# A fused cross-attention and feed-forward block on one core: the scores of batches 3 to 7 from fp16 parts

## What is computed

```python
def attention(k, v, q, Wk, Wv, bv, Wq, bq, Wo, bo):
    kp = k @ Wk.T;  vp = v @ Wv.T + bv;  qp = q @ Wq.T + bq
    probs = softmax(qp @ kp.T / sqrt(512))
    return probs @ vp @ Wo.T + bo
def ffn(x, w_gate, w_up, w_down):          # fp4(.): blocks of 16 rounded to the FP4 grid, scaled back
    h = silu(fp4(x) @ fp4(w_gate).T) * (fp4(x) @ fp4(w_up).T)
    return fp4(h) @ fp4(w_down).T
x = x + tanh(g_xattn) * attention(ctx, ctx, layernorm(x), ...)
x = x + tanh(g_ffn) * ffn(layernorm(x), ...)
```

## Time and profile before

| | |
|---|---|
| time, median of 3 runs (lowest to highest) | 863.45 us (861.89 to 864.26) |
| the profiled execution: its own time | 863.36 us |
| its span | 861.6 us |
| busy: PE, DVE, ACT, POOL | 850.2, 677.5, 375.3, 361.2 us |
| granted TensorE clock | 1.000 over the span |

### The profile page before, as it was taken

The page is one execution under the profiler, slowest core; times in us unless marked ns, Lnnn a source line. Parts: engine busy times, 40 slices in busy tenths (PEclk is TensorE's granted clock), DMA queues, the critical chain, the costliest instruction groups (busy, mean ns, idle before and its releaser), DMA issues.

```text
span 861.6 us, 11647 instructions
## 1 busy us (share of the span) xinstructions
PE 850.2 (99%) x4252; PEld 443.5 (51%) x4252; DVE 677.5 (79%) x1056; ACT 375.3 (44%) x661; POOL 361.2 (42%) x364
## 2 busy tenths in 40 slices
PE   8999999999999999999999999999999999999998
PEld 4566555544554455445544455445544554444443
DVE  5997989798988977878688858886787778877753
ACT  3666484643543344434443444334533544333320
POOL 4495448355543343334233433343333433333321
PEclk9999999999999999999999999999999999999999
DMA  9723110054334332622252225322332323333222
GB/s 308 275 71 114 27 50 14 14 120 103 70 85 104 59 59 46 130 59 58 51 114 54 59 42 124 66 58 59 64 78 58 47 60 75 60 58 64 59 46 70
DMA packets 149408, 67.45 MB, mean 78 GB/s; under 512 B 133108, under 2 KB 134502, under 8 KB 149352
## 3 DMA queue, kind: packets, MB, share of 16 engines
q1 hardware_dynamic: 149351, 66.72, 33.6%
HBM read 22.76 MB, written 8.39 MB: 36 GB/s over the span
## 4 chain that ended last, share of the span: by engine, by line
PE 69%; DVE 2%; issue 2%; ACT 1%; POOL 1%; DMA 0%; SPq 0%; POOLq 0%; ACTq 0%
PE banks L1505 44%; PE banks L1615 22%; PE banks L1499 1%; PE banks L1580 1%; PE banks L1579 1%; DVE arena L1081 0%; DMA arena<-h_parts 0%; DVE scal L1156 0%; DVE arena L1079 0%; POOL arena L527 0%; DVE stats L1121 0%; ACT h_parts L809 0%; ACT xn L735 0%; DVE ring L1243 0%; DVE h_parts L1238 0%
## 5 line engine op out<-in xcount | busy, mean ns | idle before, releaser
L1505 PE MATMUL banks<-wgu_hi,x_T 128*128 128x512 f16 (+1 forms) x1536 | 440.9, 361 | 0.0
L1505 PE MATMUL banks<-wgu_lo,x_T 128*128 128x512 f16 (+1 forms) x768 | 277.5, 361 | 0.0
L1615 PE MATMUL banks<-wd,arena 128*128 128x512 f16 x1056 | 234.6, 379 | 0.5 <-DMA arena<-h_parts 0.5
L1505 PEld LDWEIGHTS banks<-wgu_hi,x_T 128*128 128x128 f16 x1536 | 150.3, 98 | 153.4 <-issue 1.0
L1615 PEld LDWEIGHTS banks<-wd,arena 128*128 128x128 f16 x1056 | 103.3, 98 | 120.4 <-issue 0.9
L527 POOL TENSOR_TENSOR arena<-arena,h_r 128x1024 f32<-128x1024 f32 (+1 forms) x60 | 96.5, 1609 | 117.5 <-DVE h_r L1033 117.5
L527 POOL TENSOR_TENSOR arena<-arena,h_s 128x1024 f32<-128x1024 f32 x64 | 90.2, 1410 | 120.3 <-issue 89.4
L797 ACT ACTIVATE arena<-banks,scal 128x512 f32<-128x512 f32 (+1 forms) x96 | 62.1, 647 | 133.7 <-PE banks L1505 133.6
L1505 PEld LDWEIGHTS banks<-wgu_lo,x_T 128*128 128x128 f16 x768 | 75.1, 98 | 77.0 <-issue 1.3
L527 POOL TENSOR_TENSOR xwork<-xwork,x_s 128x512 f32<-128x512 f32 x32 | 33.9, 1059 | 174.3 <-DVE xwork L1081 174.3
L1079 DVE SCALAR_TENSOR_TENSOR arena<-arena 128x384 f32<-128x384 bf16 (+1 forms) x67 | 66.3, 989 | 26.2 <-ACT arena L676 26.2
(11 more groups left out here) (156 smaller groups left out, 949.9 us busy)
## 6 DMA issues: line engine op xcount, KB each, us to landing
ring<-in_x_dram SPq DMA_DIRECT2D x8, 1024.0 KB, 5.7
out_dram<-ring SPq DMA_DIRECT2D x32, 256.0 KB, 2.0
arena<-in_L_ffn_w_down_dram SPq DMA_DIRECT2D x4, 704.0 KB, 4.1
arena<-in_L_ffn_w_gate_dram SPq DMA_DIRECT2D x5, 512.0 KB, 10.8
arena<-in_L_ffn_w_up_dram SPq DMA_DIRECT2D x5, 512.0 KB, 11.0
ring<-in_L_xattn_Wk_dram SPq DMA_DIRECT2D x4, 256.0 KB, 6.0
ring<-in_L_xattn_Wq_dram SPq DMA_DIRECT2D x4, 256.0 KB, 6.8
wd<-in_ctx_dram SPq DMA_DIRECT2D x1, 1024.0 KB
```

The costliest lines, as they stand in the source:

```text
L1505: ended = e.matmul(at, l, r, start=(i == 0), stop=(i == len(terms) - 1))
L1615: ended = e.matmul(down_ps(t)[:, :], l, r, start=(k == 0 and i == 0), stop=(k == KH - 1 and i == 2))
```

## The change

From batch 3 on (`CUT = 3`) the layer norm's result and the keys are split in fp16 high and low parts, and the scores are made of high times (high, low) and low times high. What it does, engine by engine:

- PE: `att_turn` is gone for batches 3 to 7 (20 tiles). `att_scores` of such a tile is eight fp16 matmuls: four of 154 columns (the high part of xn against the keys' high and low columns side by side) and four of 77 columns (low against high). They stand in s = 1 alone: tile 0 at a1, 1 at a2, 2 and 3 at a3, in banks 5 and 6. `att_values` alternates banks 7 and 5. One transpose and one spread matmul are added in iteration 6 for the keys' power of two.
- ACT: `xn_copy` is replaced by `xn_high` (a cast of 128x512 from SBUF); the normed rows are made two tiles at a time. Once, in iterations 6 and 7: four `key_high` (128x385) and four `key_back` (128x770).
- DVE: `xn_low` per tile (two in s = 0, two in s = 1); `softmax` has two operations that read PSUM where it had one; once, `key_tops` (iteration 5, 4 x 385 columns), `key_power` (iteration 6), four `key_low` (iteration 7). `softmax` is moved ahead of `h_round(t, 0)`, and `prob_low` to the end of s = 1.
- SP: four `xn_turn` per batch, two behind `x_turn` in s = 0 and two ahead of `x_turn` in s = 1. In every iteration of the loop `x_turn(t+1)` now stands ahead of `h_turn(t-1)`, and `stack_values` at the end of s = 1.
- DVE, POOL and ACT: x's statistics and `x_apply` are moved up by one tile, from the head of iteration t+1 to the tail of iteration t, as `x_stats(t+2)` and `x_apply(t+2)`.

Semaphores of the four power-of-two steps are merged (`max_made`, `pow_made`, `pow_spread`, `pow_ready`), and `probT` becomes a view of `prob_bytes`. The core of the diff:

```diff
+        CUT = 3
+        xn_parts = [xn1[:, i, :].bitcast(F16) for i in range(2)]
+        def key_parts(b, k):
+            return keyq[:, k, b * KEYS:(b + 1) * KEYS].bitcast(F16)
...
+            def xn_turn(b, i):
+                m = cut_tile(b, i)
+                w.wait_ge(xn_lo, m + 1)
+                w.wait_ge(score_mm, b * TILES + i - 1)
+                e.dma_start_transpose(xn_T[i % 2][:, :, :], xn_parts[i % 2]).then_inc(xn_moved[i % 2], 16)
...
             for t in range(4, NT):
+                attention_part(t, "first")
                 store(t - 3)
-                attention_part(t)
-                if t == 4:
+                turn_part(t, 1)
+                if t + 1 < NT:
                     x_turn(t + 1)
+                turn_part(t, 0)
                 h_turn(t - 1)
-                if 4 < t < NT - 1:
-                    x_turn(t + 1)
+                attention_part(t, "end")
...
+            def xn_high(b, i):
+                m = cut_tile(b, i)
+                w.wait_ge(xn_made, b * TILES + i + 1)
+                if i < 2:
+                    w.wait_ge(att_mm, TILES * b)
+                else:
+                    w.wait_ge(*xn_there(b, i - 2))
+                e.copy(xn_parts[i % 2][:, 0:D], xn1[:, 2 + i % 2, :]).then_inc(xn_hi, 1)
...
                 attention_part(t, "a3")
                 h_squares(t, 0)
+                if t + 2 < NT:
+                    x_apply(t + 2)
                 attention_part(t, "a4")
...
+                if b < CUT:
+                    e.tensor_tensor(prob[:, :, :], sc, kb, ALU.add).then_inc(score_in, 1)
+                else:
+                    of_parts = banks[:, 5 * BANK:7 * BANK].rearrange("p (i n) -> p i n", i=TILES)
+                    e.scalar_tensor_tensor(prob[:, :, :], of_parts[:, :, 0:KEYS], k_fold, kb, ALU.mult, ALU.add).then_inc(*step())
+                    w.wait_ge(dve_step, step.n)
+                    e.scalar_tensor_tensor(prob[:, :, :], of_parts[:, :, KEYS:2 * KEYS], k_fold, prob[:, :, :], ALU.mult, ALU.add).then_inc(score_in, 1)
...
+            def xn_low(b, i):
+                w.wait_ge(xn_hi, cut_tile(b, i) + 1)
+                parts = xn_parts[i % 2]
+                e.tensor_tensor(parts[:, D:2 * D], xn1[:, 2 + i % 2, :], parts[:, 0:D], ALU.subtract).then_inc(xn_lo, 1)
...
+            def key_tops():
+                w.wait_ge(key_sb, 2 * KEYS_HALF)
+                e.tensor_reduce(k_tops, keyq[:, :, CUT * KEYS:ROWS], axis=AX_X, op=ALU.max, apply_absolute_value=True).then_inc(*step())
...
+                if b == CUT - 1 and (s, at) == (1, "d soft"):
+                    key_tops()
+                    prob_low(b)
+                elif b == CUT - 1 and (s, at) == (3, "a1"):
+                    values(b, 2)
+                    key_low(0)
+                    key_low(1)
...
+                elif b >= CUT and (s, at) == (0, "mid"):
+                    xn_low(b, 0)
+                    xn_low(b, 1)
+                elif b >= CUT and (s, at) == (1, "a2"):
+                    xn_low(b, 2)
+                    xn_low(b, 3)
...
                 else:
                     finish(t - 3)
                     h_round(t - 1, 1)
-                    if more and t > 5:
-                        x_stats(t + 1)
+                    if more:
+                        x_scales(t + 1)
                     attention_part(t, "d stats")
                     attention_part(t, "a1")
-                    if more:
-                        x_scales(t + 1)
                     hidden(t, 0)
...
                 attention_part(t, "a3")
                 h_scales(t, 1)
-                if t == 4:
+                if t + 2 < NT:
                     x_stats(t + 2)
+                attention_part(t, "soft")
                 h_round(t, 0)
...
             def att_scores(b, i):
+                if b >= CUT:
+                    at = 5 + i // 2
+                    if i % 2 == 0:
+                        take(at, (score_in, b + 1))
+                    w.wait_ge(k_parts, KD)
+                    w.wait_ge(*xn_there(b, i))
+                    c = i % 2 * BANK // 2
+                    for k in range(KD):
+                        e.matmul(bank[at][:, c:c + 2 * KEYS], xn_T[i % 2][:, k, :], key_parts(b, k), start=(k == 0), stop=False)
+                        ended = e.matmul(bank[at][:, c:c + KEYS], xn_T[i % 2][:, KD + k, :], key_parts(b, k)[:, 0:KEYS], start=False, stop=(k == KD - 1))
+                    ended.then_inc(score_mm, 1)
+                    return
```

More of the change, by code:

```diff
@@ L271, in build @@
             b, s = t // TILES + 1, t % TILES
-            xn = [("xn", b * TILES + i) for i in range(TILES)] if b < NBATCH else []
+            xn = [("xn", b * TILES + i) for i in range(TILES)] if b < CUT else []
+            turns += [("k_top", 0), ("k_pow", 0)] if (b, s) == (CUT - 1, 2) else []
             if t < 3:
@@ L474, in stack_values, with turn_part, attention_part @@
                 e.dma_start(under[KEYS - LEFT:2 * KEYS - LEFT, :], v_hi).then_inc(v_stacked, 16)
-            def attention_part(t):
+            def xn_turn(b, i):
[3 more added lines that the diff above has]
+                e.dma_start_transpose(xn_T[i % 2][:, :, :], xn_parts[i % 2]).then_inc(xn_moved[i % 2], 16)
+            def turn_part(t, s):
+                b = t // TILES + 1
+                if CUT <= b < NBATCH and t % TILES == s:
+                    xn_turn(b, 2 * s)
+                    xn_turn(b, 2 * s + 1)
+            def attention_part(t, at):
                 b, s = t // TILES + 1, t % TILES
                 if STACKED <= b < NBATCH:
-                    if s == 2:
+                    if (s, at) == (1, "end"):
                         stack_values(b)
+                    elif (s, at) == (2, "first"):
                         p_turn(b)
@@ L814, in attention_part @@
                     return
-                if (s, at) == (0, "d apply"):
+                if b == CUT - 1 and (s, at) == (2, "d soft"):
+                    key_high(0)
+                    key_high(1)
+                elif b == CUT - 1 and (s, at) == (3, "a2"):
+                    key_back(0)
+                    key_back(1)
+                    key_high(2)
+                    key_high(3)
+                elif b == CUT - 1 and (s, at) == (3, "a3"):
+                    key_back(2)
+                    key_back(3)
+                elif b >= CUT and (s, at) == (0, "d apply"):
+                    xn_apply(b, 0)
+                    xn_apply(b, 1)
+                    xn_high(b, 0)
+                    xn_high(b, 1)
+                elif b >= CUT and (s, at) == (1, "a1"):
+                    xn_apply(b, 2)
+                    xn_apply(b, 3)
+                    xn_high(b, 2)
+                    xn_high(b, 3)
+                elif b >= CUT and (s, at) in ((0, "a3"), (0, "a4"), (1, "a2")):
+                    return
+                elif (s, at) == (0, "d apply"):
                     ln1_apply(b)
@@ L1531, in down_subtract, with top_turn, power_spread @@
                              wd_hi[:, ks[0]:ks[-1] + 1, r * P:(r + 1) * P], start=False, stop=True, skip_group_check=True).then_inc(d_less, 1)
-            def top_turn(name, top, made, out, seen):
-                take(turn_bank[name, 0], (seen, 1))
-                w.wait_ge(made, 1)
+            def top_turn(name, top):
+                at = turn_bank[f"{name}_top", 0]
+                take(at, (pow_made, NTH[name]))
+                w.wait_ge(max_made, NTH[name])
                 n = top.shape[0]
-                e.transpose(bank[turn_bank[name, 0]][0:1, 0:n], top, ident[0:n, 0:n]).then_inc(out, 1)
-            def power_spread(name, power, made, out, seen):
-                take(turn_bank[name, 0], (seen, 1))
+                e.transpose(bank[at][0:1, 0:n], top, ident[0:n, 0:n]).then_inc(max_turned, 1)
+            def power_spread(name, power):
+                at = turn_bank[f"{name}_pow", 0]
+                take(at, (pow_ready, NTH[name]))
                 w.wait_ge(consts, ONES)
-                w.wait_ge(made, 1)
-                e.matmul(bank[turn_bank[name, 0]][:, 0:1], ones[:, :], power, start=True, stop=True).then_inc(out, 1)
+                w.wait_ge(pow_made, NTH[name])
+                e.matmul(bank[at][:, 0:1], ones[:, :], power, start=True, stop=True).then_inc(pow_spread, 1)
             def down_turn(r):
```

173 lines of the change are left out of this document (123 added, 50 removed).

## The result

| | before | with the change |
|---|---|---|
| median of the executions (lowest to highest) | 863.85 us (861.89 to 864.26, 4) | 850.55 us (850.15 to 851.05, 4) |
| profiled execution, its span | 863.36, 861.6 us | 850.62, 848.8 us |
| granted TensorE clock over the span | 1.000 | 0.998 |
| busy PE, DVE, ACT, POOL | 850.2, 677.5, 375.3, 361.2 | 835.3, 706.2, 377.0, 398.7 |

The ratio is 0.9851, 95% interval [0.9834, 0.9868]: faster by 1.5%. The forecast was 847.2 us with 843.8 to 855.0 as its range. So direction and range held, but of the 16.2 us forecast for the profiled execution 12.7 came.

The account below looks back on a forecast made before the run. The prediction took PE to bound the kernel, busy 850.2 of 861.6 us at full clock. Its sum was 863.36 - 25.7 + 9.6 + 0.3 - 0.35 = 847.2 us, with a range of 843.8 to 855.0.

Parts of the forecast that it names:

- PE is the bound, and what leaves it is gained: PE, iteration 4 to the last down: time taken off PE leaves the kernel; turn and scores of 20 tiles, 25.7 us.
- The narrow matmuls: PE, scores of batches 3 to 7: eight fp16 matmuls per tile cost 0.48 us, 9.6 us for 20 tiles.
- the fp16 load's pitch: PE, new scores: a weight load paces at 0.054 us, hidden by 154-column matmuls (0.065) but not by 77-column ones.
- The lower end by columns: PE, new scores: columns alone set the pace, 0.39 us per tile, 7.8 us for 20 tiles.
- The first rival: PE, new scores: whole weight loads pace the narrow matmuls, 0.78 us per tile, 15.7 in all, 853.3 us; chance 0.2.
- The wait in iteration 5: PE: the old 1.35 us wait goes, a new 1.0 us one comes one matmul group earlier; 0.35 us gained.
- The keys' split falls in idle time: ACT and DVE, iterations 5 to 7: eight ACT and about six DVE operations, once, fit in both engines' idle time.
- The keys' power: PE: the added transpose and spread for the keys' power of two take 0.3 us together.
- My own case: Whole kernel: the predictor's main expectation, 844.2 to about 849.5 us, given a chance of 0.66.
- the figure at 81 ns per matmul: PE, new scores: the skill's sustained pace at 128 columns gives 0.65 us per tile, 850.6 us.
- What must stay hidden in the loop: DVE, SP, ACT in iterations 12 and 13: added work and transposes stay covered; x_turn spare 3.7 us, xn_turn 4.0 and 5.8.
- The transposes of xn late: PE, first scores of s = 1: slow transfers make PE wait 4.0 us per batch, 20 us, 867; chance 0.04.

Follow-up runs that it names:

- the kernels with two banks: The change with batch 2's value products in banks 5, 7, 5, 7 instead of bank 5 alone, plus other edits: 844.36 to 845.45 us with the keys' split later, else 847.69.
- the two mixes: The change plus iteration 4's copy before x_apply(6), eight filler matmuls, later power spread, batch 2's values in banks 5, 7, 5, 7: keys' split later 844.36 to 845.45 us, unmoved 847.69.
- the copy first: The change with ACT's x_apply(6) behind the copy of xn's second tile in iteration 4, not ahead of it: 849.11 us, ratio 0.9827.
- the gap filled: The change with eight matmuls nobody reads put in iteration 0, where PE waits 1.76 us for ACT's copy of wd: 850.18 us, ratio 0.9838.
- both and the later split: The change with x_apply(6) behind xn's second copy, eight filler matmuls in iteration 0, and the keys' split and power spread one to two places later: 848.4 us, ratio 0.9818.
- the second bank: The change with the value products of batch 2 in banks 7 and 5 in turn, where they all used bank 5: 853.1 us, ratio 0.9869.
- the three groups: The unchanged kernel before, run beside the follow-up kernels: 863.05 us beside the first four, 864.39 beside the next four, 863.19 beside the last three.

## Why the prediction was right, and where its sum was off

- **PE is the bound, and what leaves it is gained.** Right. Iteration 12 was to last 14.26 + 7.13 = 21.39 us; the first `gate_up` stands at 388.63 and that of iteration 13 at 410.02, 21.39. PE's busy time fell by 14.9 us, above the 9 that were set as the mark for being wrong.
- **The narrow matmuls, 9.6 us.** Mis-sized by 1.4 us to the good side: 0.41 per tile and not 0.48, 8.2 for the twenty. The term at fault is the fp16 load's pitch, set at half of the fp32 one's, 0.054; two loads with records of 98 ns and matmuls of 67 and 35 ns go by in 0.10. The lower end by columns (0.39) was nearly the value. The first rival, 0.78 per tile, is out.
- **The wait in iteration 5, -0.35.** The mechanism was right (old wait gone, a new one at the scores before), its size wrong: +1.3. The term at fault is "its statistics take 1.44", a duration read where the neighbours were others. In the new place, beside h's rounding on DVE, they took 3.26. These 1.8 us more cover the 1.65 us of the miss.
- **"The keys' split falls in idle time."** Wrong in iteration 7, where PE lost 1.6 us to a wait that the sum had at nothing. ACT was idle on average, but the two `key_high` came right before the copy that DVE waited for, and behind DVE stood a PSUM bank that PE needed. The split alone doesn't make the wait: it is absent from the change with the statistics in their old place, from the kernel before with the move alone, and from the kernels with two banks. So the moved statistics and bank 5 used twice running are conditions of it; the share of `key_high`, about 1 us, is read from DVE's idle time, and no run takes it out by itself. The share of idle time was no proof; the queue behind the instruction had to be followed to PE.
- **The keys' power, 0.3.** 0.45; the spread cost 0.34, not 0.22.
- **Nothing was charged for the clock.** The prediction took 2.4 GHz in every slice as given. A dip behind a wait that is there in both kernels cost 1.7 us. The shorter prologue of that execution gave 1.0 back, which is luck and no gain of the change; 0.7 was left.
- **The range held in part by luck.** My own case was 844.2 (its terms give 844.4) to about 849.5, and 850.55 lies outside it. The range reached to 855 for the sake of dear narrow matmuls, and these came out at the cheap end; waits and clock, which the sum had at nothing, filled the room. That the figure at 81 ns per matmul was 850.6 is a coincidence: a pair of them would take 0.16, and it took 0.10.
- **What must stay hidden in the loop.** Held. x's transpose was issued at 403.07 and landed 3.2 us later (median), 3.7 before its use, just the forecast spare; both transposes of xn, issued from 405.40 on, land after 2.7 (4.1 was taken), long before the scores at 412.61. DVE's wait of 3.38 us is gone. Its load was underrated: two `xn_low` took 3.02 us and not 1.25. The first starts 0.4 us after a POOL multiply of 2.25 us and lasts 2.42 us, in each of the five batches; the second, and those of s = 1, last 0.68. DVE is busy 20.29 of 21.38 us where 19.5 was worked out. So it came closer to being the bound than was said.
- **The transposes of xn late.** They weren't, but the run without the moved statistics shows this mechanism at work: six waits, 0.8 us each. The prediction had priced it by slow transfers; there it was ACT's order.

The sum of the corrections: -1.4 (narrow) +1.65 (iteration 5) +1.6 (iteration 7) +0.15 (power) +0.7 (clock and lead) +0.7 (last landing) = +3.4, and 847.2 becomes 850.6 where the profiled execution had 850.62.

## What to carry to other kernels

Moving work within an engine's queue changes its price: read a duration from where the neighbours on the other engines are those of the new place, POOL's small operations above all. For each once-only piece of work put into "idle" time, follow the next instruction of the same queue to the engine that is the bound, down to the PSUM bank it frees. And when waits are taken away, look at the longest that are left: here a dip of TensorE's clock went with some of them. Side by side, none of four executions of the change ran at 1.000, five of seven of the kernel before, and six of seven of the two mixes, which have no wait above 1.51 us in their profiles.

## What the runs showed of the hardware

- **The clock falls at single waits of 1.7 to 2.8 us, in some executions.** The eleven traces that have such waits of PE have 19 of them. At ten the clock falls to 0.50, from 0.6 us before the wait's end to 1.6 us behind it: near 142 us in the change, 260 with the copy first, 231 with the gap filled, 281 with both and the later split, three times with the second bank. It isn't certain: the kernel before had its 1.74 us wait at a clock of 1.00, and the change its 2.55. In the change a dip cost 1.7 us (2.37 to 4.06 us for the same matmuls). Spans of one kernel sort by the clock: 848.0, 850.8, 851.7, 852.2 at 1.000, 0.996, 0.994, 0.994. Behind waits up to 1.5 us no dip followed in these traces, falls after PE's last matmul aside. Single executions below 1.000 are no mark of the change either: the kernel before had 2 of 13, 6 of 9 and 2 of 7 in the three groups; with the move of the statistics alone, which makes one wait longer (2.5 for 1.35), it was 6 of 10 beside the 2 of 13. Why one execution falls and another not stays open. The Trainium skill (TensorE: Matmul & The Clock Gate, "What's actually happening") says that a gate passes half or all of the pulses by how busy PE has been; the two levels seen here, 0.50 and 1.00, agree.
- **Operations of POOL on 128 x 1 elements that start while DVE rounds 128 x 1024 (a read of two SBUF tiles) last until DVE is through.** They go from 0.23 and 0.21 to 1.08 and 1.17 us and end 0.07 to 0.09 us after DVE's instruction, in all 45 such records of the change; beside DVE's one-input reduce the third operation took 0.57 as elsewhere. It goes the other way too: DVE's `xn_low`, a subtraction of two SBUF tiles, takes 2.42 us instead of 0.68 when it starts beside a POOL multiply, and ends 0.55 us after it. The Trainium skill (GPSIMD Engine Reference, Key points) says that GpSimd shares its SBUF interfaces with VectorE, with contention for DVE instructions with two SBUF inputs; the trace agrees. That it is the shared interface and not something else of these instructions was not isolated.
- **Weight loads with records of 98 ns don't slow matmuls of 67 and 35 ns**: 0.10 us per pair of loads and matmuls, unchanged when the number of pairs was doubled.
